# Causal mask by affine selects on GpSimd behind the exponential, in place of mask matmuls on TensorE

## The reference

```python
q, k, v = (proj(Wq, bq), proj(Wk, bk), proj(Wv, bv))      # tanh(x @ W + b), heads of 64
alpha = jnp.einsum('bhqd,bhkd->bhqk', q, k) / jnp.sqrt(jnp.float32(d))
causal = jnp.tril(jnp.ones((s, s), dtype=bool))
alpha = jnp.where(causal, alpha, jnp.finfo(jnp.float32).min)
alpha = jax.nn.softmax(alpha, axis=-1)
ctx = jnp.einsum('bhqk,bhkd->bhqd', alpha, v)
```

## Time and profile before

| | |
|---|---|
| median of 3 runs | 463.94 us |
| the profiled execution: time, span | 467.87 us, 466.1 us |
| TensorE busy (matmul) | 401.8 us, 86% |
| VectorE busy | 315.9 us, 68% |
| ScalarE busy | 248.1 us, 53% |
| GpSimd busy | 206.7 us, 44% |

### The profile page before, as it was taken

The page is one execution under the profiler, slowest core; times in us unless marked ns, Lnnn a source line. Parts: engine busy times, 40 slices in busy tenths (PEclk is TensorE's granted clock), DMA queues, the critical chain, the costliest instruction groups (busy, mean ns, idle before and its releaser), DMA issues.

```text
span 466.1 us, 11355 instructions
## 1 busy us (share of the span) xinstructions
PE 401.8 (86%) x4614; PEld 301.9 (65%) x4614; DVE 315.9 (68%) x833; ACT 248.1 (53%) x369; POOL 206.7 (44%) x175
## 2 busy tenths in 40 slices
PE   1689899239899999999999999999999987788992
PEld 0556577115678888587877587877587864345771
DVE  5789655734999776489799379799379793453321
ACT  2111454005787778377778377778377750224541
POOL 6565154702554344154444267443257443030546
PEclk9999999856999999999999999999999998989997
DMA  7912642180000000000000010000010000116531
GB/s 210 367 47 76 176 143 91 35 293 5 1 1 3 1 3 4 0 25 1 3 2 2 7 30 8 9 2 1 7 30 9 9 1 25 52 39 170 158 102 36
DMA packets 25372, 25.46 MB, mean 55 GB/s; under 512 B 2664, under 2 KB 21551, under 8 KB 25048
## 3 DMA queue, kind: packets, MB, share of 16 engines
q1 hardware_dynamic: 21424, 18.33, 13.2%
q0 software_dynamic: 2304, 4.25, 2.8%
q10 hardware_dynamic: 1592, 2.14, 1.3%
HBM read 16.72 MB, written 9.58 MB: 56 GB/s over the span
## 4 chain that ended last, share of the span: by engine, by line
PE 59%; DVE 24%; issue 6%; DMA 4%; POOL 3%; ACT 1%; ACTq 1%; another core or an unknown queue 1%; DVEq 0%; POOLq 0%; SPq 0%
PE sc L795 8%; DVE Pl L1245 6%; PE pj L764 6%; PE sc L663 6%; PE pj L672 6%; DVE Ph L1240 6%; PE tT L844 4%; PE cx L827 4%; PE cx L829 3%; PE pj L774 3%; PE cx L828 3%; PE tT L606 3%; PE pj L795 2%; PE sc L788 1%; POOL out L361 1%
## 5 line engine op out<-in xcount | busy, mean ns | idle before, releaser
L795 PE MATMUL sc<-Tq,Tk 64*128 64x128 f32 (+2 forms) x640 | 78.6, 345 | 0.0
L827 PE MATMUL cx<-Vh,Ph 128*128 128x65 f16 x640 | 65.8, 196 | 10.7 <-DVE cn L1254 6.1
L1240 DVE CAST Ph<-Pf 128x1024 f16<-128x1024 f32 (+1 forms) x48 | 49.7, 1035 | 29.9 <-ACT Pf L551 29.8
L795 PEld LDWEIGHTS sc<-Tq,Tk 64*128 64x128 f32 x640 | 62.3, 187 | 11.6
L827 PEld LDWEIGHTS cx<-Vh,Ph 128*128 128x128 f16 x640 | 58.6, 98 | 16.6 <-DVE cn L1254 7.9
L828 PE MATMUL cx<-Vl,Ph 128*128 128x64 f16 x640 | 65.5, 194 | 0.0
L829 PE MATMUL cx<-Vh,Pl 128*128 128x65 f16 x640 | 65.3, 194 | 0.0
L828 PEld LDWEIGHTS cx<-Vl,Ph 128*128 128x128 f16 x640 | 59.0, 99 | 0.3
L829 PEld LDWEIGHTS cx<-Vh,Pl 128*128 128x128 f16 x640 | 59.1, 98 | 0.0
L462 ACT ACTIVATE hT<-sc,RT 128x320 f32<-128x320 f32 x64 | 33.8, 528 | 34.1 <-PE sc L663 21.7
L382 POOL TENSOR_TENSOR Vl<-Tv,Vh 128x512 f16<-128x512 f32 x16 | 19.2, 1201 | 68.7 <-ACT Vh L543 68.6
(11 more groups left out here) (224 smaller groups left out, 1041.2 us busy)
## 6 DMA issues: line engine op xcount, KB each, us to landing
W<-in_L_ffn_w SPq DMA_DIRECT2D x32, 256.0 KB
disp<-empty SPq DMA_DIRECT2D x2, 1320.0 KB, 7.4
XE<-disp SPq DMA_DIRECT2D x18, 132.0 KB, 2.5
X<-xmid SPq DMA_DIRECT2D x4, 256.0 KB, 4.2
out<-X SPq DMA_DIRECT2D x4, 256.0 KB
XR<-disp SPq DMA_DIRECT2D x18, 33.0 KB, 2.2
X<-in_L_attn_states SPq DMA_DIRECT2D x2, 256.0 KB, 3.3
X<-in_L_attn_states SPq DMA_DIRECT2D x1, 512.0 KB, 5.3
```

Of the source, the lines that this page charges most:

```text
L795: m = mm(score_bank(h, c)[:, o + x:o + y], Tk[u][half(h), q:q + P], Tq[u][half(h), q + x:q + y], start=False, stop=last and (c, h) != (2, 0))
L827: mm(cx[:, o:o + HD + 1], Ph[u][:, h, a:a + P], Vh[u][:, kt, h, :], start=kt == 0, stop=False)
L1240: dve.tensor_copy(Ph[u][:, :, at], Pf[u][:, :, at]).then_inc(S["p_hi"], 1)
```

## The change

The eight mask matmuls of a pair and their two constants (`identb`, `maskn`) go. The matmul that opens a bank now clears it (`start`), and the score matmuls, which were cut so that columns with and without mask were apart, are merged: eight per pair in place of fourteen (with two of the mask matmuls counted, ten in place of sixteen), over the same columns. GpSimd gets a new function `mask`: it waits for the exponential of a chunk and writes zero above the diagonal of each diagonal block of both heads, in place in `Pf`, one affine select of 128 x 2 x 128 for each key block, four per pair, and raises `masked`. VectorE's casts wait for `masked` in place of `exp_done`.

```diff
@@ gpsimd
-            pool.memset(identb[:], 0.0).then_inc(S["pool_const"], 1)
-            pool.memset(maskn[:], 0.0).then_inc(S["pool_const"], 1)
...
+            def mask(s, u, c):
+
+                a, n, kts = CHUNKS[c]
+                pool.wait_ge(S["exp_done"], 3 * s + c + 1)
+                for kt in kts:
+                    block = Pf[u][:, :, KOFF[kt]:KOFF[kt] + P]
+                    last = pool.affine_select(out=block, in_=block, compare_op=ALU.is_ge, fill=0.0, base=0,
+                                              pattern=[[0, 2], [1, P]], channel_multiplier=-1)
+                last.then_inc(S["masked"], 1)
+
...
                 if between:
                     between()
                 if score:
+                    for c in range(3):
+                        mask(i - 1, 1 - u, c)
                     p_low(i - 1, 1 - u)
@@ tensor, scores
-                for c, (a, n, kts) in enumerate(CHUNKS):
-                    if c == 2 and project:
-                        pe.wait_ge(S["tk"], s + 2)
-                    for h in range(2):
-                        for kt in kts:
-                            o = KOFF[kt] - a
-                            mm(score_bank(h, c)[:, o:o + P], identb[:], maskn[:], start=kt == kts[0] and not (c == 2 and h),
-                               stop=False)
...
                 for h in range(2):
-                    part(h, 0, 0, P, GN)
...
+                    part(h, 0, 0, GN, True, True)
+                if project:
+                    pe.wait_ge(S["tk"], s + 2)
+                part(0, 2, 2, 2 * P, True, True)
+                part(1, 1, 1, 3 * P, True)
+                part(0, 1, 1, 3 * P, True)
+                part(1, 1, 3, P, False, True)
+                part(0, 1, 3, P, False, True)
                 pe.wait_ge(S["s_ps"], 6 * s + SCORED.index((2, 0)) + 1)
...
+                part(1, 2, 2, 2 * P, False, True)
@@ vector
             def p_high(s, u, c):
                 at = scored(s, u, c)[0]
-                dve.wait_ge(S["exp_done"], 3 * s + c + 1)
+                dve.wait_ge(S["masked"], 3 * s + c + 1)
```

More of the change, by code:

```diff
@@ L56 @@
 EPS = 1e-5
-NEG = -30000.0
 LN_PSHIFT = float(np.log(16.0))
@@ L125, in macaron @@
         identf = sb("identf", [P, P], F32)
-        identb = sb("identb", [P, P], BF16)
         onesb = sb("onesb", [P, P], BF16)
         lower = sb("lower", [P, P], BF16)
-        maskn = sb("maskn", [P, P], BF16)
         pick = sb("pick", [P, E], F32)
@@ L212, in macaron @@
             q_ps k_ps v_ps tq tk tv v_hi v_lo
-            s_ps exp_done p_hi p_lo_v p_lo_p ctx_ps rden_ready ctxn ct_ps ct_ready wo_ps yt yt_ps x_added
+            s_ps exp_done masked p_hi p_lo_v p_lo_p ctx_ps rden_ready ctxn ct_ps ct_ready wo_ps yt yt_ps x_added
             x_hi x_lo""".split()
@@ L314, in _ @@
             pool.memset(identf[:], 0.0).then_inc(S["pool_const"], 1)
-            pool.memset(identb[:], 0.0).then_inc(S["pool_const"], 1)
             pool.memset(onesb[:], 1.0).then_inc(S["pool_const"], 1)
-            pool.memset(maskn[:], 0.0).then_inc(S["pool_const"], 1)
             pool.memset(lower[:], 1.0).then_inc(S["pool_const"], 1)
[L319 to L324, removed]
+            pool.wait_ge(S["pool_const"], 3)
+            pool.affine_select(out=identf[:], in_=identf[:], compare_op=ALU.not_equal, fill=1.0, base=0,
+                               pattern=[[-1, P]], channel_multiplier=1)
             pool.affine_select(out=lower[:], in_=lower[:], compare_op=ALU.is_ge, fill=0.0, base=0,
@@ L332, in _ @@
             pool.memset(empty[:], 0.0).then_inc(S["pool_const"], 1)
-            pool.wait_ge(S["pool_const"], 6)
+            pool.wait_ge(S["pool_const"], 4)
             pool.iota(empty[:, :, NUM:WT].bitcast(U32), [[1, SLOTS // P], [1, 1]], base=NTOK,
@@ L781, in scores, with part @@
                     pe.wait_ge(S["exp_done"], 3 * s)
-                for c, (a, n, kts) in enumerate(CHUNKS):
-                    if c == 2 and project:
-                        pe.wait_ge(S["tk"], s + 2)
-                    for h in range(2):
-                        for kt in kts:
-                            o = KOFF[kt] - a
-                            mm(score_bank(h, c)[:, o:o + P], identb[:], maskn[:], start=kt == kts[0] and not (c == 2 and h),
-                               stop=False)
                 pe.wait_ge(S["tq"], s + 1)
                 pe.wait_ge(S["tk"], s + 1)
-                def part(h, c, kt, x, y, last=False):
+                def part(h, c, kt, n, first=False, last=False):
                     o, q = KOFF[kt] - CHUNKS[c][0], P * kt
-                    m = mm(score_bank(h, c)[:, o + x:o + y], Tk[u][half(h), q:q + P], Tq[u][half(h), q + x:q + y],
-                           start=False, stop=last and (c, h) != (2, 0))
+                    m = mm(score_bank(h, c)[:, o:o + n], Tk[u][half(h), q:q + P], Tq[u][half(h), q:q + n],
+                           start=first, stop=last and (c, h) != (2, 0))
                     if last:
@@ L800, in scores @@
                 for h in range(2):
-                    part(h, 0, 0, P, GN)
[L802 to L810, removed]
+                    part(h, 0, 0, GN, True, True)
[6 more added lines that the diff above has]
+                part(0, 1, 3, P, False, True)
                 pe.wait_ge(S["s_ps"], 6 * s + SCORED.index((2, 0)) + 1)
-                part(1, 2, 2, 0, P)
-                part(0, 1, 3, 0, P, True)
-                part(1, 2, 2, P, 2 * P, True)
+                part(1, 2, 2, 2 * P, False, True)
             def context(c, u, h):
```

## The result

The changed kernel takes 486.72 us (median of 4 runs, 485.49 to 487.17) against 464.13 us before: a ratio of 1.0506, 95% interval 1.0467 to 1.0546. It is 22.6 us slower by the medians. The profiled execution's span went from 466.1 to 483.8 us, 17.7 us; the difference to 22.6 is that the profiled execution of before lies 0.8% over its median and the one of after 0.25% under.

A forecast was written before the change was run, and what follows sets the result against it. TensorE bounds the attention before, the port shared by GpSimd and VectorE after (6.65 + 1.7 = 8.3 us per pair). Terms -1.4, +7.2, +8.8, +13.2, +3, -0.4 give +30.4 on 463.9: 494 us, range 469 to 515.

The forecast's parts named there:

- the port-bound case: Main forecast, 74%: selects overfill the resource GpSimd and VectorE share, 8.3 us per pair against steps of 7.45; 494 us.
- TensorE gains 0.45 per pair, its own step becomes 7.0: TensorE, plain step: mask matmuls removed save 0.60 us, coarser score pieces cost 0.15.
- A select is 0.42: GpSimd: each affine select of 128 x 2 x 128 takes 0.42 us, 1.7 us per pair.
- A select excludes VectorE fully: Shared port: selects exclude VectorE's casts and subtractions; by the memset's behaviour instead, about 10 us less.
- Casts longer, subtractions too: Sign on VectorE: casts of 128x1024 with means above the 1.0 of now, and longer subtractions.
- TensorE's waits rise from 7.8 to about 40: Sign at the first context matmul: TensorE's total wait goes from 7.8 us to about 40, for VectorE's Pl.
- The steps with the output projection gain 0.45: Three steps of 14.3 us, output projection ahead of the scores: selects hidden, TensorE gains 0.45 each, -1.4 us.
- Plain steps 8.65, +1.2: Six plain steps of 7.45 us: 8.65, between hand schedules 8.3 (VectorE first) and 9.0 (turn-taking); +7.2 us together.
- Eleven steps that VectorE already bounded, +1.2 each: Steps where VectorE was already last, at about 8.3 us: nearly the whole 1.7 of selects added, +13.2 together.
- Eleven others with more work on TensorE, +0.8 each: Steps of 7.8 to 8.2 us where TensorE had more work: +8.8 us together.
- Five inverse deviations, +0.6 each, 3 us: Five steps where selects stand behind an inverse deviation awaiting VectorE's statistics: up to 1.5 us new chain, +3 together.
- Masks hide, 455 us: Rival, 6%: selects hardly exclude VectorE, so the 20 steps bound by TensorE gain 0.45 each (-9), 455 us.

The follow-up runs named there:

- the half: The changed kernel with each select over one head only, 128 x 128, the other head without causal mask: 483.08 us, ratio 1.0324.
- the aside runs: The changed kernel with selects writing to a spare tile nobody reads and VectorE waiting for the exponentials: 488.24 us, ratio 1.0565.

## Why the prediction was right, and where its steps were mis-sized

The forecast was 494 us, 469 to 515, slower at 87%; 486.7 came. Right by its reason: the port-bound case is what the runs show. Its size is in part luck, since terms that were off by 10 us and more cancelled. By its steps:

- *TensorE gains 0.45 per pair, its own step becomes 7.0:* measured 6.9 to 7.0. The two terms of that gain were both off: the mask matmuls were worth 0.51 and not 0.60, and the 0.15 us for coarser pieces was wrong in kind, as fourteen and eight matmuls cannot be told apart.
- *A select is 0.42:* 0.40 alone. The 128 keep GpSimd busy for 63 us and have a mean duration of 0.57 for `Wf` and 0.47 for `Pf`, since they wait inside for VectorE.
- *A select excludes VectorE fully:* shown by the rows above, for casts and for subtractions; the half and the aside runs show the load. By the Trainium skill (SBUF — State Buffer, "SBUF: two separate sides") the one that starts first holds the pair for the whole instruction and the other fully blocks, for a GpSimd operation against a VectorE operation in a two-port mode, or against one with two SBUF inputs if the GpSimd operation reads SBUF. This trace agrees: a cast of 0.42 us took 1.38 beside a v remainder of 1.12 that began 0.03 us before it, and a select of 0.40 took 0.86 behind a subtraction.
- *Casts longer, subtractions too:* half of this sign was wrong. Casts and subtractions of 128x1024 out of `Pf`, before and after:

```profile
L1240 DVE CAST Ph<-Pf 128x1024 f16<-128x1024 f32 x32 | 43.0, 1342 | 29.9 <-ACT Pf L551 29.8
L1245 DVE TENSOR_TENSOR Pl<-Pf,Ph 128x1024 f16<-128x1024 f32 x16 | 20.4, 1275 | 0.0
```

```profile
L1232 DVE CAST Ph<-Pf 128x1024 f16<-128x1024 f32 x32 | 27.0, 844 | 33.1 <-POOL Pf L386 31.5 <-PE cx L821 1.4
L1237 DVE TENSOR_TENSOR Pl<-Pf,Ph 128x1024 f16<-128x1024 f32 x16 | 34.1, 2134 | 0.0
```

  Over both buffers the casts of this shape fell from 1.23 to 1.04 us, while the subtractions rose from 1.29 to 1.78. GpSimd's remainder, pushed back by the selects, now meets VectorE's subtraction more often and its cast less often. The run with the late remainder and no selects shows the same shift (1.02 and 1.55 us), so it comes from the order, which costs nothing by itself.
- *TensorE's waits rise from 7.8 to about 40:* 36.2, but only 14.8 of them for `Pl`. The larger part, 16.2, is at half 1 of the context, for the normalisation behind the cast of chunk 0, a place that the prediction did not have; 5.2 are for the ranks. All are VectorE's.
- *The steps with the output projection gain 0.45:* 13.8 for 14.3, three times.
- *Plain steps 8.65, +1.2:* 8.0 over i = 6 to 10, +0.6, under both of my hand schedules. This term of the sum was twice too large. In the trace the v remainder does step in before the last subtraction (at 180.9 and 189.1 us the subtraction takes 1.49 in place of 0.69, as in step 18 of before), but the next pair's first select does not, and my turn-taking schedule had both. Once in the five the debt is made good (7.3 after 8.5). Two more steps that were 7.45 before, i = 17 and 25, grew by 0.14 us each.
- *Eleven steps that VectorE already bounded, +1.2 each:* leaving out i = 2, which is counted below, the nine that I could place (i = 3, 4, 13, 16, 18, 21, 24, 26, 29) grew by 2.0 us together, +0.2 each; i = 21 even became shorter (8.4 to 7.9), as the step before had paid.
- *Eleven others with more work on TensorE, +0.8 each:* the seven of them without an inverse deviation (i = 1, 5, 14, 15, 22, 23, 30) grew by 0.6 us together, +0.1 each. Here and in the bounded steps most of the debt was simply not there: the price per step that I took from the hand schedule of a plain step did not carry over.
- *Five inverse deviations, +0.6 each, 3 us:* the worst-sized term, to the other side. The three steps r = 4 grew by 3.4, 4.4 and 4.5 us and i = 2 by 2.7. I had named the chain (selects behind the inverse deviation, behind VectorE's statistics) and put 1.5 us on it. What I left out is that VectorE reaches those statistics late, because its subtractions ahead of them are blocked as well. But the run with the order changed shows that only 3 us of this are the order; the rest is load that shows up there.
- *Masks hide, 455 us:* this rival's price was wrong as well. With the masks free the kernel stands at 0.9908, which is 460. Nineteen steps gain, 8.0 us together; the rest stand still or grow, 3.8 us together, of which i = 13, 21 and 29, behind the inverse deviations, have 1.8.

So the sum held because terms too large (plain, other and bounded steps: 7.2 + 8.8 + 13.2 = 29.2 us forecast, 3.2 + 0.6 + 2.0 = 5.8 measured) and one too small (3 forecast, 14.9 measured, in steps that also had their share of the other terms) met: 23.4 us too much and 11.9 too little, a net 11.5 of the 12.7 by which the forecast of +30.4 passed the profiled difference of 17.7.

## What to carry to other kernels

Before moving work to GpSimd, add up per step what GpSimd and VectorE both do on SBUF, not each engine's busy share: 44% and 68% looked free, while the sum was 6.65 of 7.45 us, and 1.7 us more cost 28 us of time whatever waited for it. Where the sum had been lowered first, 0.41 us more cost 4 us, and none of them in the plain steps. The way out of such a sum is ScalarE or TensorE, which kept their own pace here (the exponentials take 1.11 and 0.68 us before and after, TensorE's plain step 7.0 with the selects and 6.9 without): 0.46 us of cast moved to ScalarE gained 1.3 to 1.5% before the change and 2.2% after it. And time taken from the engine that is busy 86% is worth only what the second-longest chain leaves: 15 us of matmuls gave 4.

## What I had not expected

The granted clock of TensorE fell behind the 4 us stalls: 0.94 in the step with the stall and 0.87 in the next (rows of i = 20 and 21 of the changed kernel), which is part of that window at the 1.2 GHz level; with the selects ahead of the inverse deviation, where the idle time in i = 20 was 2.2 us, both windows have 1.00 (there the clock fell in i = 16, to 0.84). In i = 21 of the changed kernel TensorE is busy for all 7.9 us with the work that takes 7.1 in the other kernels, so a stall costs some 0.8 us once more, three times per execution. Over i = 12, 13, 20, 21, 28 and 29 TensorE is busy 4.7 us longer than in the kernel without masks, which is much of why its matmul time fell by 9 us and not by 15.

An indirect DMA on GpSimd lets a cast pass: that of 0.41 us at 285.19 lies wholly inside the DMA of 284.34 to 286.12. The subtraction at 285.63 was not so lucky, it ended 0.56 us behind the v remainder that followed the DMA. It is not the DMA alone: a subtraction of this shape at 297.04, 1.28 us behind the start of such a DMA as this one, took 0.69 us beside it, and one at 305.87 took 0.69 although a v remainder followed the DMA 0.51 us later. Why the turn went to the v remainder at 286.15 and not there, these rows can't tell.
